# The vertical recursion of the second layer on quarter arrays, with TensorE's program in two loops over a ring of four lines

## The reference, cut to what matters

```python
def step(w, b):
    def f(carry, inp):                       # conv1d: 5 taps over the line, 48 -> 48 channels
        nxt = inp + conv1d(carry, w, b)
        return (nxt, nxt)
    return f
xs = moveaxis(x, 2, 0)                       # 256 lines of (4, 48, 256)
D  = scan(step(down_w, down_b), xs[0], xs[1:])                # downwards, 255 steps
U  = scan(step(down_w, down_b), D[H-1], [D[H-3] ... D[0], D[H-1]])   # upwards, 255 steps, same weights
R, L = the same over columns with right_w and then left_w
```

## Time and profile before

| | us |
|---|---|
| median of 3 runs | 12674.14 |
| lowest and highest | 12665.86, 12674.85 |
| the profiled execution, its own time | 12669.85 |
| its span, from the first to the last instruction | 12668.1 |

### The profile page before, as it was taken

One profiled execution on the slowest core, in us unless ns is written; L12 is line 12 of the kernel. 1 busy time (PEld: TensorE's weight loads), 2 busy tenths in 40 slices (PEclk: granted clock), 3 DMA queues, 4 the chain that ended last, 5 costly groups with the idle time before them and its releaser, 6 DMA issues. The chain is left out here.

```text
span 12668.1 us, 315986 instructions
## 1 busy us (share of the span) xinstructions
PE 12261.6 (97%) x126170; PEld 8490.2 (67%) x126170; DVE 7918.5 (63%) x17482; ACT 5434.7 (43%) x11157; POOL 4647.2 (37%) x3557
## 2 busy tenths in 40 slices
PE   7999999899999999899999999999998999999999
PEld 6877444477767777555555555555556888888887
DVE  0000577533334544588888888888886777777777
ACT  0000111211123333455555555555555777777777
POOL 0000222100000045566666666666663444444444
PEclk9999999999999999899999999999998999999999
DMA  4333455783765489666666666666662222222222
GB/s 128 134 132 132 129 156 156 160 158 67 157 120 154 146 202 232 105 87 89 89 88 87 88 89 88 88 88 88 88 88 66 56 56 56 56 56 56 56 56 53
DMA packets 2310008, 1323.93 MB, mean 105 GB/s; under 512 B 1872228, under 2 KB 2219867, under 8 KB 2222959
## 3 DMA queue, kind: packets, MB, share of 16 engines
q1 hardware_dynamic: 2041484, 1201.47, 48.0%
q10 hardware_dynamic: 267232, 104.65, 3.5%
HBM read 648.72 MB, written 450.74 MB: 87 GB/s over the span
## 5 line engine op out<-in xcount | busy, mean ns | idle before, releaser
L1583 PE MATMUL l_m<-l_wa,l_pix 128*128 128x288 f32 x8192 | 2211.3, 413 | 13.5 <-DMA l_left<-k_rim_dram 13.5
L1583 PEld LDWEIGHTS l_m<-l_wa,l_pix 128*128 128x128 f32 x8192 | 1475.4, 190 | 699.5 <-issue 376.1
L1439 POOL TENSOR_TENSOR l_qkv<-l_qkv,l_copies 128x576 f32<-128x576 f32 x1024 | 1436.8, 1403 | 635.1 <-DVE l_qkv L1775 635.1
L1429 POOL TENSOR_TENSOR l_pix<-l_raw 128x516 f32<-128x516 f32 x1024 | 1216.0, 1188 | 1041.9 <-DVE l_t L1812 1017.3
L1285 PE MATMUL l1h_ps<-l1h_ring,l1h_w 96*96 96x256 f32 x6120 | 1326.7, 379 | 50.8 <-ACT l1h_ring L1233 47.2
L1056 PE MATMUL l1v_ps<-l1v_rows,l1v_w 96*96 96x256 f32 x6120 | 1326.4, 378 | 31.2 <-ACT l1v_rows L1029 31.2
L1285 PEld LDWEIGHTS l1h_ps<-l1h_ring,l1h_w 96*96 96x96 f32 x6120 | 998.7, 163 | 378.8 <-issue 47.5
L1269 POOL TENSOR_TENSOR l1h_columns<-l1h_blocks,l1h_ring 96x2048 f32<-96x2048 f32 x64 | 355.9, 5579 | 2418.8 <-DVE l1h_ring L1318 2418.8
L1056 PEld LDWEIGHTS l1v_ps<-l1v_rows,l1v_w 96*96 96x96 f32 x6120 | 990.7, 162 | 366.6 <-issue 30.3
L2093 PEld LDWEIGHTS l_e<-k_ident,l_turn 128*112 128x112 f32 x9900 | 1070.1, 133 | 173.3 <-issue 111.2
L2093 PE MATMUL l_e<-k_ident,l_turn 128*112 128x128 f32 x9900 | 1158.5, 275 | 12.4 <-ACT l_turn L2176 4.3
(11 more groups left out here) (245 smaller groups left out, 21184.4 us busy)
## 6 DMA issues: line engine op xcount, KB each, us to landing
l0a_x<-x_px_dram SPq DMA_DIRECT2D x128, 1176.0 KB, 5.2
l0b_x<-x_in_dram SPq DMA_DIRECT2D x128, 493.8 KB
l_raw<-l_raw SPq DMA_DIRECT2D x128, 483.6 KB, 7.2
l_raw<-x_dram SPq DMA_DIRECT2D x1280, 48.0 KB, 3.7
l_x<-x3p_dram SPq DMA_DIRECT2D x132, 384.0 KB
l_out<-x_dram SPq DMA_DIRECT2D x528, 96.0 KB
out_dram<-l_out SPq DMA_DIRECT2D x132, 384.0 KB
x_dram<-l0b_out ACTq DMA_DIRECT2D x256, 193.5 KB, 3.1
```

The source lines that it names most:

```text
L1429: nc.gpsimd.tensor_tensor(pix[:, n % 2, i, half * HALF:(half + 1) * HALF].rearrange("p (r w) -> p r w", w=PW), in0, in1, op).then_inc(pix_ ...
L1439: nc.gpsimd.tensor_tensor(q, q, copies[:, g % 2, 1:2, :].broadcast_to([128, 2, OUTC]), ALU.add)\
L1583: last = nc.tensor.matmul(bank[i][:, 0:OUTC], pix[:, k, i, first:first + 128], wa[:, b, i, :], start=True, stop=(i in (1, 2)))
```

## The change

The vertical stage is written anew.

- **Layout.** 112 partitions: 48 channels at partitions 0 to 47 and 48 at 64 to 111 (`side(0)`, `side(1)`). Pixels of a line stay in their order. A line lies in one of two ways, in turn. *Whole* (even places): each side holds one of the group's two images, 256 pixels. *Parted* (odd places): each side holds one half of the line of both images, 130 pixels each (128 and a halo of 2).
- **TensorE.** Five taps, weights of 48 by 48, each on one quarter of the array: 5 taps x 2 sides read (`r`) x 2 sides written (`c`) = 20 matmuls per step and group, 130 columns wide from a whole line, 128 from a parted one. A whole line gives a parted one and the reverse.
- **Loops.** TensorE's program is two loops (down, up) of 63 turns of four steps, and three steps written out behind each. For that the state is no longer in the big tile but in a ring of four lines per group (`ring_w`, `ring_p`), whose addresses repeat every four steps.
- **VectorE** writes the new line into the ring (one instruction per step and group as before, now 112 partitions, two PSUM banks) and must wait that the line four steps before has been copied out.
- **Copies.** Each line is copied from the ring into the big tiles (`whole`, `parted`): group 0 by ScalarE, group 1 by GpSimd. The transposing copies of the way up are cut into 10 parts per chunk and group and shared out in the same way, one part between two lines. ScalarE's normalizing goes in 6 parts per chunk.
- **Turning point.** The last line of the way down is parted, the first of the way up must be whole: ScalarE and GpSimd copy it over in 10 copies, and TensorE waits for them.
- **SyncE** paces its transfers: one or two per line computed. Loads come as 4 transfers of whole lines (rows of 1 KB) and 8 of parted ones (520 B) per chunk, stores as 4 and 8 likewise. Tiles are cleared (`memset`) before the first load.
- **`stage_l0_apply`** writes the pixels in their order, so its VectorE and ScalarE instructions read and write without a stride of two. The intermediate array `up` has its dimensions in another order; the horizontal stage reads it in pieces of the same size.

```diff
+        def copy_line(eng, copy, g, n):
+            at = place(n)
+            eng.wait_ge(state[g], n + 1)
+            copy(line(g, at), ring_line(g, of_phase(n))).then_inc(copied[g], 1)
+
+        def copy_up(eng, copy, g):
+            for n in range(LAST + 1, STEPS + 1):
+                h = up_step(n)
+                copy_line(eng, copy, g, n)
+                c, m = h // CH + 1, CH - 1 - h % CH
+                if c < NCH and 0 < m <= 10:
+                    turn_part(eng, copy, c, g, m - 1)
...
         @block.tensor
         def _(pe):
-            pe.wait_ge(consts, 64)
-            for n in range(1, STEPS + 1):
-                before = n - 1 if n <= LAST else 2 * LAST + 1 - n
+            pe.wait_ge(consts, 96)
+            pe.wait_ge(blank, 2)
+            def step(m, rows_there):
                 for g in range(2):
-                        pe.wait_ge(state[g], n - 1)
-                    for s in range(3):
-                        last = nc.tensor.matmul(
-                            ps[g][0:C2, 0:GI * HW2], w[:, s, :],
-                            X[:, before // CH % SL, g * GI:(g + 1) * GI, before % CH, s:s + HW2],
-                            start=(s == 0), stop=(s == 2))
-                    last.then_inc(product[g], 1)
+                    pe.wait_ge(state[g], rows_there)
+                    pe.sem_inc(stepping, 1)
+                    for t in range(TAPS):
+                        for r in range(2):
+                            for c in range(2):
+                                if m % 2 == 0:
+                                    first = t + c * (W - PART)
+                                    x, width = ring(g, m, side(r))[:, first:first + PART], PART
+                                else:
+                                    first = t + 2 * r
+                                    x, width = ring(g, m, side(r))[:, c, first:first + HW2], HW2
+                                last = nc.tensor.matmul(ps[g][side(c), r, 0:width], w[side(r), t, :], x,
+                                                        start=(t == 0), stop=(t == TAPS - 1), skip_group_check=True)
+                                if t == TAPS - 1:
+                                    last.then_inc(product[g], 1)
+            for phase in range(2):
+                if phase == 1:
+                    pe.wait_ge(kept, 10)
+                with pe.Fori(0, LAST // 4) as i:
+                    for m in range(4):
+                        step(m, i * 4 + (phase * LAST + m + 1))
+                for m in range(LAST // 4 * 4, LAST):
+                    step(m, phase * LAST + m + 1)
...
+                    if n > LAST:
+                        dve.wait_ge(copied[g], n - 4 if n > LAST + 4 else LAST)
+                    elif n > 4:
+                        dve.wait_ge(copied[g], n - 4)
+                    dve.wait_ge(product[g], 4 * n)
                     nc.vector.scalar_tensor_tensor(
-                        out=X[:, h // CH % SL, images, h % CH, 1:HW2 + 1],
-                        in0=ps[g][0:C2, 0:GI * HW2].rearrange("p (i u) -> p i u", i=GI), scalar=bias[:, 0:1],
-                        in1=x, op0=ALU.add, op1=ALU.add).then_inc(state[g], 1)
+                        out=ring_line(g, of_phase(n)),
+                        in0=ps[g][0:PP, :, 0:(HW2 if of_phase(n) % 2 == 0 else PART)], scalar=bias[:, 0:1],
+                        in1=line(g, at), op0=ALU.add, op1=ALU.add).then_inc(state[g], 1)
```

More of the change, by code:

```diff
@@ L954, in stage_l1_vertical, with side, place, ring @@
         block = ctx.enter_context(nc.Block())
+        def side(h):
+            return slice(h * HI, h * HI + C)
         def up_step(h):
             return 2 * LAST - h
[L960 to L962 removed]
+        def place(n):
+            return n if n <= LAST else 2 * LAST - n - 1
+        def ring(g, m, part=slice(0, PP)):
+            if m % 2 == 0:
+                return ring_w[part, g, m // 2 % 2, :]
+            return ring_p[part, g, m // 2 % 2, :, :]
@@ new lines, in load_x, with both @@
+                    pace(2 * i)
+                    sp.dma_start(whole[side(i % 2), k, i // 2, :, :], rows[:, 0, :, 1:W + 1])\
+                      .then_inc(loaded[k], 16)
+                    pace(2 * i + 1)
+                    for h in range(2):
+                        first = 1 + h * (W - PART)
+                        sp.dma_start(parted[side(h), k, i // 2, :, i % 2, :], rows[:, 1, :, first:first + PART])\
+                          .then_inc(loaded[k], 16)
+            def both(c, g, h):
+                for tile, kept_in in ((whole, D["down_w"]), (parted, D["down_p"])):
+                    here = tile[side(h), c % SL, g]
+                    yield here.rearrange("p r w -> p (r w)") if tile is whole else here.rearrange("p r i w -> p (r i w)"), \
+                        kept_in[h, :, c, g, :]
@@ new lines, in turn_parted, with turn_part @@
+        def turn_parted(copy, c, g, h, i, q):
+            for rows, into in rows_of_parted(c):
+                src = rows[side(h), g, :, i, 2 * h:2 * h + HW2].rearrange("p v (n u q) -> p q n v u", n=WBLK // 2, q=2)
+                last = copy(turn_p[side(h), c % 2, g, i, :, q, into, :], src[:, q])
+            last.then_inc(turned[g], 1)
+        def turn_part(eng, copy, c, g, m):
+            if m == 0:
+                eng.wait_ge(copied[g], up_step(c * CH))
+            if m == 0 and c < NCH - 2:
+                eng.wait_ge(stored[c % 2], 192 * ((NCH - 1 - c) // 2))
+            if m >= 6 and g == 1:
+                eng.wait_ge(turned[g], 10 * (NCH - 1 - c) + m)
+                eng.wait_ge(copied[g], min(up_step(c * CH) + m + 2, STEPS))
+            if m < 2:
+                turn_whole(copy, c, g, m)
+            elif m < 10:
+                turn_parted(copy, c, g, (m - 2) // 4, (m - 2) // 2 % 2, m % 2)
@@ new lines, in copy_line @@
+        def copy_line(eng, copy, g, n):
[9 more added lines that the diff above has]
+                    turn_part(eng, copy, c, g, m - 1)
+                    if m > 6 and g == 1:
+                        eng.wait_ge(turned[g], 10 * (NCH - 1 - c) + m)
+            eng.wait_ge(copied[g], STEPS)
+            for m in range(10):
+                turn_part(eng, copy, 0, g, m)
```

302 lines of the change are left out of this document (199 added, 103 removed).

## The result

The changed kernel took **12,514.16 us** in the median of four runs (12,502.38 to 12,521.05); the kernel before, beside it on the same chip, 12,672.65. The ratio is 0.9873 with a 95% interval of 0.9858 to 0.9888, so some 158 us less. Later runs of the same two kernels gave 0.9875 (0.9858 to 0.9891). The profiled execution took 12,521.05 us, 148.8 less than that of before.

The account below looks back on a forecast made before the run. The prediction took TensorE's matmuls to pace the vertical stage: -203.5 + 32 + 5 + 4 + 2 = -160.5 us from 12669.85 gives 12509, and the median 4 us above, 12,514 us. Range 12,480 to 12,600.

Parts of the forecast that it names:

- Matmuls: Vertical stage, TensorE: four quarters side by side, 1.100 us per step and group instead of 1.300, -203.5 us.
- The chain: Vertical stage: one group's own round trip takes 2.14 us and fits under both groups' 2.20 us of matmuls; nothing counted.
- rival A: Vertical stage: a round trip over 2.20 us sets the pace; at 2.35 us +77, 12,590 us; chance 0.13.
- the shorter start: In the chain: 0.06 us from semaphore to first weight load instead of 0.23, making the chain 1.97 us.
- Loop turns: TensorE's two loops of 63 turns: 0.25 us per turn for 126 turns, +32 us, range 0 to +100.
- Start, turning point, end: Vertical stage's edges: later first loads and more pieces +5, ten copies at the turn +4, later last transposing +2 us.
- Transfers: Vertical stage's loads and stores: DMA share rises from 0.75 to 0.88, costing 0, up to +15 us.
- Copies and VectorE beside GpSimd: Vertical stage: line copies fit into each chunk's 35 us and GpSimd's work does not slow VectorE's additions; 0 us.
- First layer's last stage: Stage ahead of the vertical one: VectorE's additions get shorter but TensorE idles only 4.5 us; 0 to -3 us.
- Rival B: The loop costs nothing, or transfers and start are all hidden: 12,482 us; chance 0.12.
- C: TensorE's loop body is fetched anew each turn, 3.5 us x 126: +249, 12,923 us; chance 0.05.
- D: Vertical stage: quarters run two, not four, at a time, 2.2 us per group: +920, 13,594 us; chance 0.02.

Follow-up runs that it names:

- e3: Changed kernel with the same matmuls reordered, all five taps of one quarter before the next quarter: 16,764 us.
- e12: Changed kernel with an added 64-column VectorE addition, and a wait for it, before each addition: 12,665.4 us.
- e2: Changed kernel without the outer two of five taps, 12 matmuls per step and group instead of 20 (another result): 12,391 us.
- e10: Changed kernel with eight steps in a turn of TensorE's loops instead of four: 12,505.7 us.
- e5: Changed kernel with the array `up` laid out in whole lines, so stores go in runs of 512 bytes instead of 256: 12,489.7 us.
- e9: Changed kernel with e5's 512-byte stores, small constants loaded first and the second chunk's normalizing later: 12,490.85 us median of four runs, ratio to before 0.9862.
- e11: Changed kernel with sixteen steps in a turn of TensorE's loops instead of four: 13,080 us.
- e1: Changed kernel with TensorE's vertical-stage loops written out, 510 steps and no loop: 12,965 us.

## Why the prediction was right

The mechanism was right: the matmuls gave what was forecast, and the chain fitted. That the median came out at 12,514.16 where 12,514 was forecast is luck, as the terms below show.

*Matmuls, -203.5 forecast.* -201.9 measured (1019 x 1.1017 = 1122.6 against 1324.5). Four quarters do run side by side at 130 columns; the pitch taken from the earlier trace rows was off by 1.7 ns per group. e3 shows that it depends on the order, taps outside, which the argument had not weighed.

*The chain, 2.14 us forecast, and rival A.* 2.16 by e12, 1.70 with three taps by e2 where the same sum gives 1.70. It fits under 2.20, with less room than the shorter start would have left; the sum with the longer start was the right one. Nothing is lost to it in the steady turns.

*Loop turns, +32 forecast: the term that was mis-sized.* A turn of 8 groups takes 8.813 us from branch to branch, and in e10, with half as many turns, one of 16 groups takes 17.626, exactly twice that: nothing is left for the turn. The branch lasts 0.21 us as in the earlier trace rows, but TensorE's queue had matmuls ahead, as in L869. In the trace of the changed kernel 18 to 20 matmul records of the turn have still to start when its branch begins, and in the loop of L857 before it was 20: the same number of records, not the same time. At 27.5 ns each they are 0.5 us of work here, and that was enough to cover a turn. My own sum had named 0 as the lower bound and took a quarter of a microsecond because the work queued ahead was "four times shorter in time". That reading was right (27.5 ns a record against 109), but no row said that 0.5 us would be too little.

*Start, turning point, end: +5, +4, +2 forecast.* +18.6, +4.9, +14.4 measured. The start was 7.6 before the first addition (SyncE issues the first chunk's loads until 2433.1 and only then the constants, of which the last lands at 2446.9, and the chunk's loads wait for GpSimd's and VectorE's clearing), 4.7 in the first four intervals, where ScalarE normalizes in between, and 6.3 where TensorE breaks off in its first turn, to fetch instructions. At the end I had counted the work of the copies, done 9.6 us after the last addition, but not SyncE: 4.0 to 4.8 us for each pair of stores, one after the other until 3640.6. e5's take 3.1 to 3.9, and the next stage begins 12 us sooner.

*Transfers, 0 forecast.* 6.5 us in the additions, within the "up to 15". The share was to rise to 0.88 and rose to 0.96. It isn't the size of the packets alone: before moved 61.79 MB in 128,403 packets in 400 us at a share of 0.747, after 49.14 MB in 102,801 in 300 us at 0.957, in both some 480 bytes each. So a byte takes a fifth more of the engines' time; why is open. With half the packets the waits are gone in both runs that have it, e5 and e9; without, ScalarE waited 8 to 45 us in the six others.

*Copies and VectorE beside GpSimd, 0 forecast.* No addition waited for GpSimd's copies (400 ns, ScalarE's 416); GpSimd's work beside it left VectorE's additions at 484 and 489 ns. The sixteen delays of 0.3 us, one in every 64 additions, were not foreseen; near some of them (2576.4, 2647.2, 2717.9) a packet of the instruction queue q14 comes (2578.1, 2648.9, 2716.5). That is only nearness in time, not tested.

*First layer's last stage, 0 to -3.* -4.1; 1062.8 to 1063.9 us in every run with the new code, 1067.7 before.

The profiled execution was forecast at 12,509 and took 12,521 us, of which 8 are the last stage's. It came out so near because two errors nearly cancel: 31 us too many for the loops, and some 38 too few for start, end, stores and VectorE's delays. *Rival B* had the loops right and the edges wrong; *C* is excluded by the absent packets and shown as a mechanism by e11. *D* is excluded by the pitch, though e3, at the lower clock, makes something worse than D out of the same matmuls.

## What to carry to other kernels

On quarter arrays, issue the four quarters in turn, with the accumulating taps outside, and measure by records per microsecond, since a busy TensorE tells nothing. Such a stream used its instructions faster than they came (4.6 GB/s wanted, 3.3 to 4.1 got), so the loop is not a price but a condition: its body has to fit, and doubling it is free until it doesn't. For a stage that is a recursion, work out the chain of one group before the pitch; here 0.03 us of 2.20 are left, and the next gain has to come from the chain, not from the matmuls. And a shorter stage shows its edges: the 33 us more before its first step, in its first turn and behind its last are a fifth of the 175 won in between.

## What the runs showed of the hardware

- In the written-out e1 TensorE's instructions came at 3.3 GB/s beside data transfers (100 packets of 16 KB in 500 us), some 51 loads and matmuls per us, and at 4.1 GB/s without (30 in 120 us). A body of 82 KB is held over 31 turns, one of 164 KB is not, and its branch takes 4.87 us instead of 0.21.
- A loop's first turn is fetched while it runs: in nine runs TensorE broke off at the same matmul record for 0.7 to 5.9 us, and went on 1.3 to 1.5 us after the end of an instruction packet. When a loop's branch begins, some 19 matmul records ahead of it have still to start, at 27.5 ns a record as at 109.
- With all taps of one quarter in a row (e3) TensorE is shown busy 400 of 400 us at a granted clock of 0.50 (1.2 GHz), and a record takes 417 ns instead of 269.
- A VectorE operation of one element, with no wait between, starts together with the next one (both at 2620.26 us) and costs nothing; with a semaphore between, 64 columns cost 0.32 us.
- At a DMA share above 0.95 the engines moved 164 GB/s in 478-byte packets and 179 in 880-byte ones; a pair of stores holds SyncE for 4.0 to 4.8 us then.
